# Softmax sums of a cross-attention stage: chunks of exponentials added up ahead of the sum matmuls

## The reference, cut to what matters

```
q, k, v = heads(x @ Wq.T + bq), heads(ctx @ Wk.T + bk), heads(ctx @ Wv.T + bv)
scores = clip(q @ k.T / sqrt(32), -50, 50); masked tokens count as -50 after a second clip
probs  = softmax(scores over the 375 tokens)
delta  = clip(residual_scale, 0, 0.3) * (probs @ v @ Wo.T + bo)
x      = x + layernorm(delta) * gamma + beta
```

## Time and profile before

| | |
|---|---|
| median of 3 runs | 487.19 us (485.66 to 490.10) |
| the profiled execution | 488.89 us, of it span 487.2 us |
| mean granted TensorE clock | 0.993 |
| TensorE, weight loads, VectorE | 96%, 73%, 60% of the span |
| ScalarE, POOL | 48%, 17% |
| HBM read and written | 58.76 and 14.42 MB, 150 GB/s over the span |

### The profile page before, as it was taken

One profiled execution on the slowest core, in us unless ns is written; L12 is line 12 of the kernel. 1 busy time (PEld: TensorE's weight loads), 2 busy tenths in 40 slices (PEclk: granted clock), 3 DMA queues, 4 the chain that ended last, 5 costly groups with the idle time before them and its releaser, 6 DMA issues.

```text
span 487.2 us, 10104 instructions
## 1 busy us (share of the span) xinstructions
PE 467.1 (96%) x3942; PEld 355.4 (73%) x3951; DVE 294.4 (60%) x557; ACT 235.4 (48%) x362; POOL 83.3 (17%) x105
## 2 busy tenths in 40 slices
PE   8999999999999899999999688989999999999997
PEld 6877788777877566676798566878886665556996
DVE  4964464458857887655755323777885976555111
ACT  4655433553576365463846545957755492222000
POOL 2210400005024000001071011232332252000000
PEclk9999999999999999999999988999999999999999
DMA  8999787923694145233397977867323452000111
GB/s 274 352 337 358 288 286 237 314 87 126 229 293 132 54 112 149 70 90 77 104 303 216 267 230 283 245 234 240 110 59 119 131 170 68 1 0 0 39 57 57
DMA packets 59181, 82.75 MB, mean 170 GB/s; under 512 B 20097, under 2 KB 43649, under 8 KB 57985
## 3 DMA queue, kind: packets, MB, share of 16 engines
q1 hardware_dynamic: 59136, 82.14, 53.5%
q10 hardware_dynamic: 2, 0.01, 0.0%
HBM read 58.76 MB, written 14.42 MB: 150 GB/s over the span
## 4 chain that ended last, share of the span: by engine, by line
PE 88%; DVE 7%; issue 3%; DMA 1%; ACT 1%; POOL 0%; DVEq 0%; ACTq 0%
PE psum L1536 14%; PE psum L189 13%; PE psum L187 13%; PE psum L1586 7%; PE psum L1377 6%; PE psum L1339 4%; PE psum L652 4%; PE psum L1444 4%; PE psum L1491 4%; PE psum L1322 4%; PE psum L1386 3%; PE psum L1494 3%; PE psum L1474 3%; PE psum L1503 2%; DVE e L1870 1%
## 5 line engine op out<-in xcount | busy, mean ns | idle before, releaser
L189 PE MATMUL psum<-wv_p,kv_p 128*128 128x512 f32 x288 | 76.2, 413 | 0.0
L187 PE MATMUL psum<-kv_p,wk_p 128*128 128x384 f32 x384 | 74.2, 343 | 0.0
L187 PEld LDWEIGHTS psum<-kv_p,wk_p 128*128 128x128 f32 x384 | 66.8, 188 | 2.1 <-issue 0.2
L189 PEld LDWEIGHTS psum<-wv_p,kv_p 128*128 128x128 f32 x288 | 53.7, 188 | 15.8 <-issue 3.7
L1202 ACT ACTIVATE e<-psum,mask_bias 128x448 f32<-128x448 f32 x96 | 53.9, 637 | 22.7 <-PE psum L1474 22.4
L1870 DVE TENSOR_SCALAR e<-e 128x1344 f32<-128x1344 f32 x32 | 28.8, 900 | 20.1 <-ACT e L1202 20.1
L1491 PE MATMUL psum<-e,vst 128*32 128x112 f32 x768 | 38.2, 270 | 1.6 <-issue 0.9
L1536 PE MATMUL psum<-xt,wg_b 128*128 128x448 f16 x176 | 36.9, 352 | 0.3 <-issue 0.3
L1536 PE MATMUL psum<-xt,wu_b 128*128 128x448 f16 x176 | 36.9, 352 | 0.0
L1586 PE MATMUL psum<-h_p,wd_r 128*128 x176 | 36.7, 369 | 0.0
L209 DVE SCALAR_TENSOR_TENSOR khl<-psum,bqk,khl 128x384 f16<-128x384 f32 x32 | 19.6, 613 | 27.0 <-ACT khl L199 26.8
(11 more groups left out here) (188 smaller groups left out, 815.8 us busy)
## 6 DMA issues: line engine op xcount, KB each, us to landing
kst<-k_scratch SPq DMA_DIRECT2D x32, 384.0 KB, 6.4
kv_raw<-in_ctx_feat SPq DMA_DIRECT2D x12, 768.0 KB, 5.8
w_stage<-in_w SPq DMA_DIRECT2D x6, 1408.0 KB, 8.0
cn<-in_ctx_tok SPq DMA_DIRECT2D x8, 768.0 KB, 9.6
k_scratch<-khl SPq DMA_DIRECT2D x128, 48.0 KB, 1.9
v_scratch<-vsp SPq DMA_DIRECT2D x24, 256.0 KB, 2.8
vst<-v_scratch SPq DMA_DIRECT2D x8, 768.0 KB, 4.6
qst<-qhl SPq DMA_DIRECT2D x32, 112.0 KB, 4.7
```

Of the source, the lines that this page charges most:

```text
L187: mm = pe.matmul(psum[:, kv_bank(p), 0:TP], wk_p[:, u, k, n * P:(n + 1) * P], src[:, v, k, :], **ends)
L189: mm = pe.matmul(psum[:, kv_bank(p), :], src[:, u, k, n * P:(n + 1) * P], wv_p[:, v, k, :], **ends)
```

## The change

A new set of buffers `zs[0..2]` (128x448) takes, for some groups, the sum of the three chunks of `e[g]`: chunk 0 plus chunk 1, then chunk 2 added on its 119 valid partitions. For a group in `FOLDED[b]` the 12 sum matmuls on `e[g]` are left out, and four sum matmuls on `zs[g]` stand at the end of `values(b, 3)`.

- In every element POOL adds groups 0 and 1 (`fold(b, g)` on POOL): the one ahead of `value_bias`, the other between `delta_inverse` and `x3_inverse`.
- In elements 0 to 3 VectorE adds group 2 as well, between the clips of groups 2 and 3.
- TensorE waits for POOL's four adds ahead of the new matmuls (`z_added`). ScalarE waits for the adds before it writes `e[0]` and `e[1]` again. POOL waits for the previous element's last sum matmul before it writes `zs` again.

```diff
+        zs = [at(f"zs{g}", [P, 4 * S], F32, where) for g, where in enumerate((194304, 194304 + 1792, 170240))]
+        FOLDED = [(0, 1, 2)] * 4 + [(0, 1)] * (B - 4)
...
+            def fold(b, g):
+                pool.wait_ge(e_ready, G * b + g + 1)
+                after(pool, pv_sum, G * b)
+                pool.tensor_tensor(zs[g][:], e[g][:, 0, :], e[g][:, 1, :], ALU.add).then_inc(z_added, 1)
+                pool.wait_ge(z_added, 4 * b + 2 * g + 1)
+                pool.tensor_tensor(zs[g][0:T - 2 * P], zs[g][0:T - 2 * P], e[g][0:T - 2 * P, 2, :], ALU.add).then_inc(z_added, 1)
+
+            for g in range(G):
+                pool.wait_ge(k_spilled[g], 64 * B)
             for b in range(B):
+                fold(b, 0)
                 if b:
                     value_bias(pool, b - 1)
                 if b >= 4:
                     delta_inverse(pool, b - 4)
+                fold(b, 1)
                 if b >= 4:
                     x3_inverse(pool, b - 4)
...
                 after(act, pv_sum, m - 3)
+                if b and g < 2:
+                    act.wait_ge(z_added, 4 * (b - 1) + 2 * g + 2)
+                if b and g == 2:
+                    act.wait_ge(e_ready, G * b)
...
-                    for hh in range(4):
-                        mm = pe.matmul(psum[32 * hh:32 * hh + 32, D_UZ[b][1], 0:S],
-                                       (z_pick_last if c == TC - 1 else z_pick)[:, g, :], e[g][:, c, hh * S:(hh + 1) * S],
-                                       start=(g, c) == (0, 0), stop=(g, c) == (G - 1, TC - 1))
+                    if g not in FOLDED[b]:
+                        for hh in range(4):
+                            mm = pe.matmul(psum[32 * hh:32 * hh + 32, D_UZ[b][1], 0:S],
+                                           (z_pick_last if c == TC - 1 else z_pick)[:, g, :], e[g][:, c, hh * S:(hh + 1) * S],
+                                           start=(g, c) == (len(FOLDED[b]), 0), stop=False)
+                if g == G - 1:
+                    pe.wait_ge(z_added, 4 * (b + 1))
+                    for r in FOLDED[b]:
+                        for hh in range(4):
+                            mm = pe.matmul(psum[32 * hh:32 * hh + 32, D_UZ[b][1], 0:S], z_pick[:, r, :], zs[r][:, hh * S:(hh + 1) * S],
+                                           start=False, stop=r == FOLDED[b][-1])
                 mm.then_inc(pv_sum, 1)
...
+            def fold(b):
+                chained(dve, dve.tensor_tensor(zs[2][:], e[2][:, 0, :], e[2][:, 1, :], ALU.add))
+                chained(dve, dve.tensor_tensor(zs[2][0:T - 2 * P], zs[2][0:T - 2 * P], e[2][0:T - 2 * P, 2, :], ALU.add))
...
                 clip(G * b + 2)
+                if 2 in FOLDED[b]:
+                    dve.wait_ge(e_ready, G * b + 3)
+                    fold(b)
                 if b >= 4:
                     x3_statistics(dve, b - 4)
                 clip(G * b + 3)
```

More of the change, by code:

```diff
@@ L558, in build @@
         e_ready = sem("e_ready")
+        z_added = sem("z_added")
         pv_sum = sem("pv_sum")
```

## The result

The changed kernel takes **491.01 us** (median of 22 runs, 487.30 to 493.89), the kernel before 487.87 us in 22 runs on the same chips. The ratio is 1.0074, with a 95% interval of 1.0053 to 1.0094: slower by 0.5 to 0.9%, so within 1%. The prediction was 490.1 us.

A forecast was written before the change was run, and what follows sets the result against it. TensorE's pace bounds elements 0 to 3, a VectorE loop nearly matched by TensorE elements 5 to 7. Terms -3.4 + 2.9 + 0 + 3.6 + 1.2 - 1.4 = +2.9 us on the 487.19 median gave 490.1, range 481.5 to 496.

The forecast's parts named there:

- elements 0 to 2, with the stops: First three cross attention elements: 1.15 us saved in each, -3.4 us; fewer TensorE stops in the stage, -1.4 us.
- element 3: VectorE and POOL adds taking turns delay projection 0 by 2.9 us (bounds 1.35 and 3.3).
- POOL and VectorE take turns: While POOL adds, VectorE's clips and two-input adds stand still, and the reverse; line 685 held too, delay 1.4 us.
- Rival 1: Cross attention: the adds hide, costing VectorE little; 484 us, chance 0.20.
- who comes first: Elements 5 and 6: POOL's group 1 add at 349.17 precedes VectorE's clip at 349.28, making x3 ready 1.4 us later.
- the loop: Elements 5 and 6, through projection, spread, VectorE's run and values: 14.1 us instead of 12.3, +1.8 each.
- The pair of group 0: Elements 5 and 6: POOL's adds for group 0 lie beside projection and spread, where VectorE has 1.13 us to spare.
- a POOL add: A 128x448 add with two SBUF inputs, taken as 0.94 us from value_bias, at worst 1.48; 16 pairs.
- the stops: TensorE's "issue" stops in cross attention, 9.4 us, shrink with 15% fewer instructions: -1.4 us (bounds +3 and -9.4).
- rival 2: TensorE's stops go: 7 to 10 us less, 3.4 us cover returns in elements 0 to 2; about 483, chance 0.13.
- the main case: Cross attention: POOL's adds hold up VectorE, +2.9 us in sum, 490.1 us, own range 486.5 to 494.5; chance 0.47.
- rival 3: Elements 5 to 7: TensorE waits of 2 us or more lower the clock, +5 us, 495; chance 0.20.

The follow-up runs named there:

- x3: The changed kernel with POOL's adds cut to 4 of 448 columns, all instructions, waits and matmuls kept: 480.25 us against 487.39 before, ratio 0.9876.
- x6: The changed kernel with only POOL's pair for group 0 in elements 4 to 7: 485.84 us against 486.56 for the kernel before, ratio 0.9961.
- x1: The changed kernel with adds in elements 0 to 3 only, elements 4 to 7 as before: 483.68 us against 487.39 before, ratio 0.9946.
- x8_light_keys: The kernel before with key fetches of elements 2 to 7 cut to one head of four: 482.54 us against 486.56, ratio 0.9896.
- x4: The changed kernel without VectorE's adds, group 2's sums back on TensorE: 492.15 us against 487.39 for the kernel before, ratio 1.0111.

## Why the prediction was right, and where it was not

Element by element, in the two profiled executions:

| part | predicted | measured |
|---|---|---|
| elements 0 to 2, with the stops | -4.8 | -7.6 |
| element 3 | +2.9 | +2.6 |
| element 4 | 0 | -1.1 |
| elements 5 and 6 | +3.6 | +3.6 |
| element 7 | +1.2 | +1.8 |
| sum | +2.9 | -0.7 |

**Right: POOL and VectorE take turns.** The step on which the case rested was that a VectorE instruction with two SBUF inputs, or a clip, stands still while POOL adds. x3, with adds of 4 columns, takes the effect away. It held for every such form met: clips 1.62 to 1.71 us, the transposed tile 1.62, the statement of x3 1.39, VectorE's adds 1.24 and 1.44. No row of before showed line 685, now 688, held. By the rule of the Trainium skill (SBUF — State Buffer, Who interferes with whom) on a VectorE instruction with two SBUF inputs beside a GpSimd one that reads SBUF it is held; the trace agrees, 1.39 against 0.75 us. Rival 1, that the adds hide, was wrong by this.

**Right: who comes first.** POOL's add of group 1 was expected 0.11 us ahead of the clip of group 2; it is 0.14 ahead (345.55 and 345.69). The clip was expected at 1.6 us, and is 1.71. The loop was expected at 14.1 and is 14.39. Of the other signs, projection 0 was to come some 3 us later after the reciprocal of element 2, and comes 2.2 later (11.98 against 9.77).

**Right for a partly wrong reason: the loop.** The pair of group 0 was costed at nothing, hidden beside the projection. x6 shows that it costs 0.57. In the whole change VectorE's way round the loop is 12.33 - 1.13 + 0.83 + 0.95 + 0.86 + 0.64 = 14.48 us, and that is the bound; but for the wait of 0.72 us for POOL's second inverse root, which stands in both traces, VectorE waits for nothing in it. The way over the projection, which was the predicted one, gives 12.33 + 1.50 + 0.38 = 14.21 with the measured prices. The two are 0.3 us apart, so the slip was small; the step "beside projection and spread, where VectorE has 1.13 us to spare" failed, since one POOL pair holds two VectorE instructions, 1.78 us. Element 7 was short of about as much (1.2 expected, 1.8 measured; 0.7 in x6, where the pair of group 0 stands alone).

**Mis-sized: a POOL add.** Taken as 0.94 us from value_bias. Where POOL comes first it takes 1.12 to 1.16; the second of a pair, in its turn behind a VectorE instruction, 1.39 to 1.69. The Trainium skill (GPSIMD Engine Reference, Engine selection) has GpSimd at about twice VectorE's time for two inputs, which with VectorE's 0.63 makes an estimate of 1.26: the measured first add is between that and value_bias.

**Mis-sized: the stops.** They were taken to fall with the number of instructions in the stage, 1.4 of 9.4 us. With 24 of 48 sum matmuls gone in elements 0 to 3 they fell by 7.3 (10.3 to 3.0), by 6.1 in x1 alone; they are waits for instruction transfers (x8_light_keys). In time, 3.4 and 1.4 had been expected of elements 0 to 2, and 7.6 came; by the five kernels that share these elements it is 5.0 to 7.6. "Issue" stops under 4 us were named as the sign of rival 2, which had 0.13 of the chance, and that sign came. Its time, 483, did not. That time leaves out the 7.7 us that the main case has for elements 3 and 5 to 7; with them the rival's own figures give 490.1 + 1.4 + 3.4 less 7 to 10, 485 to 488. Its other half, that the cover goes with the stops, is seen in element 3, where TensorE waits 2.94 us for the clip in front of group 3.

**Not typical: the two traces.** By the traces the change is 1.0 us faster, by the medians 3.1 slower. Of the 4.1 between them, 1.0 is that the profiled execution of before stands above its median (488.89 and 487.87), and 3.1 that the one of the changed kernel stands below its own. The clock has only a small part in this. Of the changed kernel's 22 executions 7 have a mean clock of 0.996 or above, 489.4 us on average, and 14 of 0.990 or below, 491.6 us. The profiled one, at 0.996, took 487.89, so it is 1.5 below its like. At equal clock the kernels stay apart: the 69 executions of the kernel before that were timed beside the experiments took 486.4 us on average at 0.995 or above and 487.8 at 0.988 to 0.991, where the changed kernel has 489.4 and 491.2. These 69 were 0.9 us faster on average than the 22 beside the changed kernel, so some 2.3 us of the difference stand at equal clock, and the mean clocks, 0.991 and 0.993, are worth about half a microsecond by these groups. What rival 3 feared is seen in x4's trace, 1.05 and 1.59 us in two projections, and not in the changed kernel's. Elements 0 to 2 are part of the rest: 34.0 us in this trace, where the same program has 35.1 on average.

So that the sum came within 1 us of the measured time is in part luck, by terms that offset each other: 3.6 us of gain too few in the sum over the elements (-0.7 instead of +2.9), and 3.8 us by which the medians differ more than the elements do in the two traces. The mechanism of the loss was right, and its size in elements 3, 5 and 6 right within 0.3 us each. Where the 3.1 us of the medians lie, element by element, one trace of each kernel can't show.

## What to carry to other kernels

An idle GpSimd isn't free room: each of its adds here held the clip or the VectorE instruction with two SBUF inputs that it met, while VectorE instructions that read PSUM went on. Such a pair is worth moving only where VectorE has more slack than the delay of both instructions that it holds (1.13 us against 1.78 here). Apply such an offload by stage, not everywhere: here adds in three elements of eight made the kernel 1.0% faster (0.8% by the medians), and with those in the other five the whole was 0.7% slower. Where a stop of an engine covers other work, count its cover as gone when the stop goes. And before a trace is read against a median, see how far the one execution stands from its like: here the two traces had the wrong sign.

## What the runs showed of the hardware

- TensorE's stops without a releaser end 1.2 to 1.6 us after a 16 KB transfer of instructions has landed (43 of 46). A sixth of the sum matmuls taken out (8 net of 48 in an element) shortened three elements by 3.0 us where their pace gives 3 x 0.38 = 1.1; cutting the key fetches (DMA share 1.05 to 0.65) took 4.5 us of the stops at equal work.
- The clock is not a function of the program alone: the mean is 0.986 to 1.000 in 22 executions of the changed kernel, and the same wait of 2.3 us on VectorE was followed by a projection of 3.02 us in one kernel's trace and 4.61 in another's.
- An add of two SBUF operands of 448 columns on GpSimd took 1.12 us where it came first, value_bias of the same size 0.93, an add on 119 partitions in turn with VectorE 1.39 to 1.69.
- Beside such an add VectorE's reciprocal from PSUM (0.86) and its statistics with one SBUF input (0.69) kept their length; clips went from 0.79 to 1.62 and line 685 from 0.75 to 1.39.
